# A four-layer graph network on one core: the source stage's three engine orders rewritten, its attribute scans parted, and the attributes' mean moved to the destination stage

## The chip, the core and the metric

The kernel runs on one core of a Trainium2 chip. The core has five instruction streams: TensorE (PE; its weight loads are listed apart as PEld), VectorE (DVE), ScalarE (ACT), GpSimd (POOL) and SyncE (SP, which here only issues DMA transfers). Each stream runs in its own order and waits for the others through semaphores. The metric is the device time of one execution in microseconds (us), lower is better.

## The reference, cut to what matters

There are 100,000 nodes with 128 features, and 50,000 edges sorted by destination. Four layers follow each other; after each of them `x = layernorm(x + layer(x))`.

```python
# layer 1: three hops over the edges, then one matrix
Z1 = spmm(x); Z2 = spmm(Z1); Z3 = spmm(Z2)      # segment_sum(w[:, None] * Z[src], dst)
x  = layernorm(x + concat(x, Z1, Z2, Z3) @ W0 + b0)
# layer 2: an MLP fed with each node's edge attributes (48 columns)
out1 = segment_sum(attr, dst)
out2 = where(has, segment_max(attr, dst), 0)
out3 = out1 / maximum(cnt, 1)                   # the mean
h    = relu(concat(x, out1, out2, out3, u) @ W1 + b1)
x    = layernorm(x + (h @ W2 + b2 + x))
# layer 3: attention over the edges with a skip matrix; layer 4: one weighted hop
```

A node with no incoming edge has zeros in Z1 to Z3 and in out1 to out3; only nodes that are some edge's destination need the attribute terms.

## The kernel before, in words

All work goes in groups of 512 rows (T = 4 tiles of 128). The 50,000 edges make EG = 98 groups; SL = 4 buffer slots `s` are used in turn, and one loop iteration covers four groups, so the edge loops have EI = 25 iterations. The helper `steps(eng, n, (stage, lag), ...)` writes one engine's program: in every step, for group g, it issues each stage in the order listed, for group g minus that stage's lag. So the lists given to `steps` are the hand-written order of each engine, and one "step" is one group.

The program runs through these stages, one after another: an index preparation; the node stage, in which all 100,000 nodes go through the layers as if they had no edges, while the first two hops run beside it; the **source stage** (98 groups), where the third hop is made and nodes that have edges get layers 1 to 3 in their role as sources, and the attribute sums and maxima are made by running scans; the **destination stage** (98 groups, in reverse order), where layer 2 is made again with the attributes for destination nodes; the attention; and the last hop with the output.

In the source stage, for group g:

- POOL (line 803) gathers 4 x 128 rows of the second hop into `gat` (`z_gather(2)`) and 4 x 128 rows of the input into `xg` (`x_gather`). The buffers have four slots; a gather waits for PE to have turned the tile of four groups before. After the last gather POOL issues 44 scatters of a code table (`codes`, line 804), and then, after waits for the X1 stores, starts the gathers of the destination stage (`dst_gather`).
- DVE (lines 2032 to 2034) weighs the gathered rows (L1924), scans them (`z_scan`, L1945, in from PSUM), sums squares for three layer norms (`power`, L1897), applies them (`norm`, L1909 and L1912), makes the second residual (`layer2`, L1979), and treats the attributes: the running sum (L2020), the running maximum (L2022), both in `attr_scan`, and the mean (`attr_mean`, L2029).
- PE (lines 1148 and 1149) turns tiles (L970) and multiplies: `chain_b1` and `chain_d1` turn the first and second normed tile, `z_turn` and `x_turn` the gathered ones, `chain_a` is the four-part product of layer 1 (L1020, L1025), `chain_b2` and `chain_c` the MLP (L1065, L1080), `chain_d2` the skip product (L1123).
- ACT (lines 1369 to 1371) makes squares (L1265), square roots (L1279), relu (L1336), copies out of PSUM (L1255) and PSUM seeds (L1244).
- SP loads the two earlier hops, row masks and attributes (`attr_load` has four transfers, one of them the row `inv` of reciprocal counts), and stores the three normed tiles, ATT (sums and maxima) and MNT (means).

In the destination stage PE multiplies the turned rows, ATT and MNT by three parts of W1 in one accumulation (`chain_b2("d")`, L1065, L1067, L1068). DVE's list there is line 2057, SP's loads are `att_load`.

The two DVE lines of the attribute scans, which depend on the group before through the last column:

```python
dve.tensor_tensor_scan(att_e[s][0:AF, :], f2B[s][0:AF, :], atr_e[s][0:AF, :],
                       att_e[s - 1][0:AF, G - 1:G], ALU.mult, ALU.add)
dve.tensor_tensor_scan(att_e[s][AM:AK, :], fmB[s][AM:AK, :], atr_e[s][AM:AK, :],
                       att_e[s - 1][AM:AK, G - 1:G], ALU.min, ALU.max)
```

## Time and profile before

| what | value |
|---|---|
| time, median of 3 runs | 6279.33 us (6278.2 to 6283.3) |
| the profiled execution's own time | 6277.28 us |
| its span, first to last instruction | 6275.5 us |
| mean granted TensorE clock | 0.875 of full speed |
| busy: PE, DVE, ACT, POOL | 4503.8, 4371.1, 3114.7, 4344.4 us |
| source stage: first gather to last gather on POOL | 1993.6 to 3066 us |
| destination stage: first gather on POOL | 3127.0 us |

The profile tells for each engine which instructions ran when, and, for idle time just before an instruction, which event ended it ("<-releaser"; "issue" means that it waited for nothing that the profile shows). A group's "mean ns" is the mean duration of one instruction. DVE instructions overlap a little at their ends, so what one costs on DVE is read from start to start.

### The profile page before, as it was taken

The page shows a single profiled execution, that of the slowest core. Times are in us where ns is not written, and L with a number is a line of the kernel's source. Part 1 is how long each engine was busy: PE and PEld are TensorE (multiplying, and loading weights), DVE is VectorE, ACT ScalarE, POOL GpSimd, SP SyncE. Part 2 cuts the span into 40 slices and gives each one's busy share as a digit, 9 for nine tenths or more (in the row PEclk, how much of TensorE's full clock was granted, in tenths as well). Part 3 has the DMA queues.
Part 4 walks back from the last instruction along what each step waited for, and adds up shares of the span by engine and source line. Part 5 has one row for each costly group of instructions (what it writes and reads, how often), then busy time and mean ns, then how long its engine had stood idle before and what let it go on. Part 6 is the DMA issues. An engine that isn't in the chain of part 4 may idle for free. (4 is left out here: it accounts for less than half of the span.)

```text
span 6275.5 us, 102230 instructions
## 1 busy us (share of the span) xinstructions
PE 4503.8 (72%) x25328; PEld 3191.3 (51%) x25328; DVE 4371.1 (70%) x8168; ACT 3114.7 (50%) x6471; POOL 4344.4 (69%) x4339
## 2 busy tenths in 40 slices
PE   1079899997886999999889999978887884432200
PEld 0057688886665777777744444444444442211100
DVE  8966799987886888888733334369999995753300
ACT  0057688885664555555533333348888883110000
POOL 0056677777777777777766666657777776777777
PEclk9999999999999999999999999988888885555555
DMA  1033588887897999999755555534444446953311
GB/s 30 7 87 109 169 250 248 252 239 226 283 287 218 257 262 263 263 262 263 212 163 164 167 165 163 164 113 115 113 115 115 115 116 204 328 171 96 96 42 40
DMA packets 896637, 1090.56 MB, mean 174 GB/s; under 512 B 137109, under 2 KB 543521, under 8 KB 895492
## 3 DMA queue, kind: packets, MB, share of 16 engines
q1 hardware_dynamic: 757158, 816.08, 43.4%
q0 software_dynamic: 137984, 221.55, 13.8%
q10 hardware_dynamic: 1344, 51.38, 2.1%
q14 instruction: 113, 0.93, 0.0%
q8 instruction: 38, 0.62, 0.0%
HBM read 652.84 MB, written 497.99 MB: 183 GB/s over the span
## 5 line engine op out<-in xcount | busy, mean ns | idle before, releaser
L970 PE MATMUL bank<-ident,gat 128*128 128x128 f32 x2352 | 430.5, 312 | 627.7 <-DVE zT L1945 551.5
L1080 PE MATMUL bank<-W2s,hT 128*128 128x128 f32 x6272 | 777.1, 277 | 77.6 <-ACT hT L1336 77.6
L1065 PE MATMUL bank<-x1T,W1x 128*128 128x512 f32 x1568 | 773.1, 605 | 30.5 <-ACT x1T L1255 26.9
L1080 PEld LDWEIGHTS bank<-W2s,hT 128*128 128x128 f32 x6272 | 733.9, 192 | 103.6 <-ACT hT L1336 102.2
L970 PEld LDWEIGHTS bank<-ident,gat 128*128 128x128 f32 x2352 | 298.3, 161 | 776.2 <-issue 582.5
L1265 ACT ACTIVATE mbuf<-t 128x512 f32<-128x512 f32 x490 | 310.1, 633 | 711.2 <-DVE t L1979 440.8
L1336 ACT ACTIVATE hT<-bank,b1u 128x512 f32<-128x512 f32 x784 | 491.4, 677 | 245.2 <-PE bank L1068 236.3
L1924 DVE TENSOR_TENSOR gat<-gat,pays 128x512 f32<-128x512 f32 x392 | 270.6, 690 | 425.5 <-DMA gat<-X,pays 366.5
L970 PE MATMUL bank<-ident,x 128*128 128x128 f32 x3136 | 487.1, 278 | 107.6 <-DVE x L1912 84.9
L722 POOL DMA_INDIRECT gat<-X,d_x x392 | 392.8, 1002 | 222.2 <-issue 222.2
L735 POOL DMA_INDIRECT Y<-x,d_out x392 | 405.0, 1033 | 176.4 <-issue 116.4
L970 PEld LDWEIGHTS bank<-ident,x 128*128 128x128 f32 x3136 | 366.4, 142 | 313.3 <-DVE x L1912 169.6
L722 POOL DMA_INDIRECT gat<-X,s_src x392 | 402.5, 1027 | 161.9 <-issue 161.6
L722 POOL DMA_INDIRECT gat<-Z2E,pays x392 | 416.2, 1062 | 121.0 <-issue 120.7
L1945 DVE TENSOR_TENSOR_SCAN zT<-fB,zT,bank 128x512 f32<-128x512 f32 x392 | 498.2, 1271 | 2.2 <-PE bank L970 2.2
L722 POOL DMA_INDIRECT x<-in_x_rows,s_src x392 | 415.9, 1061 | 119.5 <-issue 119.5
L722 POOL DMA_INDIRECT gat<-in_x_rows,pays x392 | 378.2, 965 | 148.5 <-issue 117.5
L756 POOL DMA_INDIRECT VQ<-s_v,s_q x392 | 396.4, 1011 | 119.4 <-issue 119.4
L722 POOL DMA_INDIRECT gat<-X,pays x392 | 385.2, 983 | 129.3 <-issue 118.6
L749 POOL DMA_INDIRECT pays<-PAY,s_q x392 | 373.1, 952 | 146.3 <-issue 109.3
L722 POOL DMA_INDIRECT gat<-Z1E,pays x392 | 377.8, 964 | 119.6 <-issue 100.3
L2046 DVE TENSOR_TENSOR zT<-bank,ffB 128x512 f32<-128x512 f32 x98 | 67.8, 692 | 540.8 <-PE bank L970 540.8
(366 smaller groups left out, 11529.4 us busy)
## 6 DMA issues: line engine op xcount, KB each, us to landing
X<-x SPq DMA_DIRECT2D x588, 256.0 KB, 3.0
fB<-row_s_same SPq DMA_DIRECT2D x392, 256.0 KB
Y<-x SPq DMA_DIRECT2D x294, 256.0 KB, 3.8
xT<-in_x_fm SPq DMA_DIRECT2D x196, 256.0 KB
ffB<-rows_last_notlast SPq DMA_DIRECT2D x98, 512.0 KB
out_rows<-Y ACTq DMA_DIRECT2D x28, 1792.0 KB, 10.4
Z1T<-zT SPq DMA_DIRECT2D x98, 256.0 KB
Z1E<-zE SPq DMA_DIRECT2D x98, 256.0 KB
```

What stands on the lines that cost most here:

```text
L722: pool.indirect_dma_start(out=tile[:, t, 0:width], out_offset=None, in_=table, in_offset=bass.IndirectOffsetOnAxis(ap=index[t], axis=0)).t ...
L735: pool.indirect_dma_start(out=table, out_offset=bass.IndirectOffsetOnAxis(ap=index[t], axis=0), in_=rows[t], in_offset=None, bounds_check= ...
L749: pool.indirect_dma_start(out=pays[:, c, :], out_offset=None, in_=PAY, in_offset=bass.IndirectOffsetOnAxis(ap=s_q[:, c:c + 1], axis=0)).th ...
L756: pool.indirect_dma_start(out=VQ, out_offset=bass.IndirectOffsetOnAxis(ap=s_q[:, c:c + 1], axis=0), in_=s_v[:, c:c + 1], in_offset=None, b ...
L970: mm = pe.transpose(dst[:, t, :], tiles[t], ident[:, :])
L1065: mm = pe.matmul(bH[h][:, :, :], W1x[:, cols], x1T[s][:, :], start=True, stop=kind != "d")
L1080: mm = pe.matmul(bMLP[:, t, :], hT[h][s][:, t * P:(t + 1) * P], W2s[:, h, :], start=False, stop=h == HC - 1, skip_group_check=True)
L1265: act.activation(sq[k % 3][s % 2], [bT1, t2[s], bSK, t2[s]][k][:, :, :], ACT.Square).then_inc(S(f"squared{k}", s), 1)
L1336: a = act.activation(hT[h][s][:, :], flat(bH[h]), ACT.Relu, bias=b1u[:, h:h + 1])
L1924: dve.tensor_tensor(gat[s][:, :, 0:P], gat[s][:, :, 0:P], pays[:, bass.ds(g, T), 1].bitcast(F32).rearrange("p (t a) -> p t a", a=1).to_bro ...
L1945: dve.tensor_tensor_scan(zT[s][:, :], fB[s][:, :], flat(bIN), zT[s - 1][:, G - 1:G], ALU.mult, ALU.add).then_inc(S("scanned", s), 1)
L2046: dve.tensor_tensor(zT[s][:, :], flat(bTR), f2B[s][:, :], ALU.mult).then_inc(S("x2sel", s), 1)
```

## The change

The source stage is given new orders on PE, ACT and DVE; the two scans of `attr_scan` become two stages (`attr_scan` for the sum, `attr_max` for the maximum) with `layer2` between them; `norm2` moves from the start of the next step (lag 4) to the end of its step (lag 3), ahead of the third norm. The mean is no longer made, stored (MNT) or fed (`inv`) in the source stage: the destination stage loads the row `inv` in place of MNT, into the buffers of `x1`, and makes the mean there (`att_mean`). SP waits for all X1 stores before the destination loads. The list of the whole change, lines that only renumber a semaphore's base included:

```diff
@@ -83,10 +83,10 @@
 
         AFTER = {
             "ld_z": ("ld_x", NI * 16), "ld_x2d": ("ld_z", EI * 32),
-            "ld_last": ("ld_attr", EI * 64), "ld_own": ("ld_x2d", EI * 32),
+            "ld_last": ("ld_attr", EI * 48), "ld_own": ("ld_x2d", EI * 32),
             "st_x2d": ("st_zT", EI * 32), "st_att": ("st_z2", 2 * EI * 16),
             "decayed": ("x2d", EI), "centred": ("attr_sums", EI),
-            "delta": ("attr_mean", EI), "t3": ("x2sel", EI), "fin_sum": ("agg", EI),
+            "delta": ("att_mean", EI), "t3": ("x2sel", EI), "fin_sum": ("agg", EI),
             "q_mm": ("skip", NI + EI), "k_mm": ("x2_turned", NI + 2 * EI), "v_mm": ("hidden", NI + 2 * EI),
             "alpha": ("mlp", NI + 2 * EI), "skip_e": ("x1_turned", NI + 2 * EI), "agg_turned": ("mm1", NI + EI),
             "q_out": ("x1T", NI + 2 * EI), "decay": ("relu", NI + 2 * EI), "weight": ("x2T", NI + EI),
@@ -123,7 +123,6 @@
         Y = dram("Y", [N_X + E_PAD, P])
         ZT = [dram(f"Z{k}T", [P, E_PAD]) for k in (1, 2)]
         ATT = dram("ATT", [AK, E_PAD])
-        MNT = dram("MNT", [AF, E_PAD])
         X2DT = dram("X2DT", [P, E_PAD])
 
         PAIRS = {p: dram("rows_" + "_".join(p), [2, E_PAD]) for p in (
@@ -267,6 +266,7 @@
 
         att, mnt, atr = ([flat(a) for a in z] for z in zin)
         x2d = fB
+        inv_d = [flat(x) for x in x1s]
         xg, atr_e, att_e = x4, atr, [flat(z) for z in zE]
         xs, qT, prod, dlt, dec, elt = x1T, hT[0], hT[1], att, mnt, atr
         aw, av, den, agg, aggn, own = [flat(t) for t in xT], f2B, zT, [flat(t) for t in zE], x2T, xT
@@ -582,22 +582,20 @@
 
 
             def attr_load(i, s):
-                if void(sp, i, s, ("ld_attr", i, 64)):
+                if void(sp, i, s, ("ld_attr", i, 48)):
                     return
                 g = i * SL + s
-                reuse(sp, "st_att", s, i, 32)
+                reuse(sp, "attr_sums", s, i)
                 sp.dma_start(atr_e[s][0:AK, :], attr_fm[:, epos(g)]).then_inc(S("ld_attr", s), 16)
                 row_load(f2B[s], ROWS["same"], g, S("ld_attr", s), 0, AF)
                 row_load(fmB[s], ROWS["samem"], g, S("ld_attr", s), AM, AF)
-                row_load(fmB[s], ROWS["inv"], g, S("ld_attr", s), 0, AF)
 
             def attr_store(i, s):
-                if void(sp, i, s, ("st_att", i, 32)):
+                if void(sp, i, s, ("st_att", i, 16)):
                     return
                 g = i * SL + s
-                ready(sp, "attr_mean", s, i)
+                ready(sp, "attr_sums", s, i)
                 sp.dma_start(ATT[:, epos(g)], att_e[s][0:AK, :]).then_inc(S("st_att", s), 16)
-                sp.dma_start(MNT[:, epos(g)], atr_e[s][0:AF, :]).then_inc(S("st_att", s), 16)
 
             all_slots(sp, "st_zT", 2 * EI * 16)
             all_slots(sp, "st_z2", 2 * EI * 16)
@@ -625,7 +623,9 @@
 
 
             all_slots(sp, "mm1", NI + EI)
-            all_slots(sp, "st_att", EI * 32)
+            all_slots(sp, "st_att", EI * 16)
+
+            all_slots(sp, "st_x1_", (NI + EI) * 16)
 
             def att_load(i, s):
                 if void(sp, i, s, ("ld_att", i, 32), ("ld_last", i, 16)):
@@ -633,7 +633,7 @@
                 g = edge_group(i, s, True)
                 reuse(sp, "hidden", s, ci("d", i))
                 sp.dma_start(att[s][0:AK, :], ATT[:, epos(g)]).then_inc(S("ld_att", s), 16)
-                sp.dma_start(mnt[s][0:AF, :], MNT[:, epos(g)]).then_inc(S("ld_att", s), 16)
+                row_load(inv_d[s], ROWS["inv"], g, S("ld_att", s), 0, AF)
                 reuse(sp, "x2d", s, i)
                 pair_load(ffB[s], ("last", "notlast"), g, S("ld_last", s))
 
@@ -1060,6 +1060,7 @@
                 prior(pe, "relu", s, c)
                 if kind == "d":
                     ready(pe, "ld_att", s, i, 32)
+                    ready(pe, "att_mean", s, i)
                 for h in range(HC):
                     cols = slice(h * P, (h + 1) * P)
                     mm = pe.matmul(bH[h][:, :, :], W1x[:, cols], x1T[s][:, :], start=True, stop=kind != "d")
@@ -1145,8 +1146,8 @@
             all_slots(pe, "z_rows", 2 * EI)
             all_slots(pe, "x2T", NI)
 
-            steps(pe, EI, (of("s", chain_b1), 2), (of("s", chain_a), 1), (of("s", chain_b2), 2),
-                  (of("s", chain_d1), 4), (z_turn(2), 0), (x_turn, 0), (of("s", chain_c), 3), (of("s", chain_d2), 4), peeled=1)
+            steps(pe, EI, (of("s", chain_b1), 2), (of("s", chain_a), 1), (of("s", chain_b2), 2), (z_turn(2), 0),
+                  (x_turn, 0), (of("s", chain_d1), 4), (of("s", chain_c), 3), (of("s", chain_d2), 4), peeled=1)
             all_slots(pe, "x2T", NI + EI)
             all_slots(pe, "x_src", EI)
             all_slots(pe, "scanned", 3 * EI)
@@ -1366,9 +1367,9 @@
                 reuse(act, "mm1", s, ci("s", i))
                 evac(xT[s][:, :, :], bBK[:, :, :], S("x_src", s))
 
-            steps(act, EI, (square("s", 0), 1), (std("s", 0), 1), (relu("s"), 2), (seed_mm1("s"), 0), (x2_out("s"), 4),
-                  (x_src, 0), (square("s", 1), 3), (seed_mlp("s"), 2), (std("s", 1), 3), (x1_out("s"), 1), (square("s", 2), 4),
-                  (std("s", 2), 4), peeled=1)
+            steps(act, EI, (square("s", 0), 1), (std("s", 0), 1), (relu("s"), 2), (x2_out("s"), 4), (x_src, 0),
+                  (seed_mm1("s"), 0), (square("s", 1), 3), (square("s", 2), 4), (std("s", 1), 3), (std("s", 2), 4),
+                  (x1_out("s"), 1), (seed_mlp("s"), 2), peeled=1)
 
             steps(act, EI, (x1_out("d"), 0), (square("d", 1), 2), (seed_mlp("d"), 1), (std("d", 1), 2), (relu("d"), 1),
                   peeled=1)
@@ -2012,30 +2013,38 @@
 
             def attr_scan(i, s):
 
-                if void(dve, i, s, ("attr_sums", i, 1)):
-                    return
-                ready(dve, "ld_attr", s, i, 64)
-                reuse(dve, "st_att", s, i, 32)
+                if void(dve, i, s):
+                    return
+                ready(dve, "ld_attr", s, i, 48)
+                reuse(dve, "st_att", s, i, 16)
                 prior(dve, "attr_sums", s, i)
                 dve.tensor_tensor_scan(att_e[s][0:AF, :], f2B[s][0:AF, :], atr_e[s][0:AF, :],
                                        att_e[s - 1][0:AF, G - 1:G], ALU.mult, ALU.add)
+
+            def attr_max(i, s):
+
+                if void(dve, i, s, ("attr_sums", i, 1)):
+                    return
+                prior(dve, "attr_sums", s, i)
                 dve.tensor_tensor_scan(att_e[s][AM:AK, :], fmB[s][AM:AK, :], atr_e[s][AM:AK, :],
                                        att_e[s - 1][AM:AK, G - 1:G], ALU.min, ALU.max).then_inc(S("attr_sums", s), 1)
 
-            def attr_mean(i, s):
-                if void(dve, i, s, ("attr_mean", i, 1)):
-                    return
-                ready(dve, "attr_sums", s, i)
-                dve.tensor_tensor(atr_e[s][0:AF, :], att_e[s][0:AF, :], fmB[s][0:AF, :], ALU.mult
-                                  ).then_inc(S("attr_mean", s), 1)
-
-            steps(dve, EI, (norm2("s"), 4), (z_weigh(2), 0), (power("s", 0), 1), (norm1("s"), 1), (z_scan(2), 0),
-                  (layer2("s"), 3), (power("s", 1), 3), (attr_scan, 0), (power("s", 2), 4), (attr_mean, 0),
+            steps(dve, EI, (z_weigh(2), 0), (power("s", 0), 1), (norm1("s"), 1), (z_scan(2), 0), (attr_scan, 0),
+                  (layer2("s"), 3), (attr_max, 0), (power("s", 1), 3), (power("s", 2), 4), (norm2("s"), 3),
                   (norm("s", 2, lambda s: bSK, x3, "ln3_out", x3_free), 4), peeled=1)
             all_slots(dve, "mm1", NI + EI)
-            all_slots(dve, "st_att", EI * 32)
+            all_slots(dve, "st_att", EI * 16)
             dve.memset(x2d[SL - 1][:, :], 0.0).then_inc(S("carry0"), 1)
             dve.wait_ge(S("carry0"), 2)
+
+            def att_mean(i, s):
+
+                if void(dve, i, s, ("att_mean", i, 1)):
+                    return
+                ready(dve, "ld_att", s, i, 32)
+                reuse(dve, "hidden", s, ci("d", i))
+                dve.tensor_tensor(mnt[s][0:AF, :], att[s][0:AF, :], inv_d[s][0:AF, :], ALU.mult
+                                  ).then_inc(S("att_mean", s), 1)
 
             def x2_select(i, s):
 
@@ -2054,7 +2063,8 @@
                 dve.tensor_tensor_scan(x2d[s][:, ::-1], fmB[s][:, ::-1], zT[s][:, ::-1], x2d[s - 1][:, 0:1],
                                        ALU.mult, ALU.add).then_inc(S("x2d", s), 1)
 
-            steps(dve, EI, (x2_select, 3), (layer2("d"), 2), (x2_carry, 3), (power("d", 1), 2), (norm2("d"), 2), peeled=1)
+            steps(dve, EI, (x2_select, 3), (layer2("d"), 2), (x2_carry, 3), (power("d", 1), 2), (att_mean, 0), (norm2("d"), 2),
+                  peeled=1)
 
 
             def att_scores(i, s):
```

## Rows read from the trace of the kernel before

**Rows 1.** The page: busy time of each engine over the span.

```profile
PE 4503.8 (72%) x25328; PEld 3191.3 (51%) x25328; DVE 4371.1 (70%) x8168; ACT 3114.7 (50%) x6471; POOL 4344.4 (69%) x4339
```

**Rows 2.** Busy time by stretch, steady source stage: PE, PEld, DVE, ACT, POOL.

```profile
core 0: us, PE busy (x) PEld busy (x) DVE busy (x) ACT busy (x) POOL busy (x), PEclk, DMA share, GB/s
2100.00:3050.00 950.00, 871.50 (x6393) 730.63 (x6392) 827.07 (x1262) 520.98 (x1092) 737.24 (x694) 1.00 0.96 263
```

**Rows 3.** Waits, 2300 to 2900 us (source stage): total us, times, longest.

```profile
PE bank L970 <- DVE x L1912: 25.1, 53, 0.6
PE bank L1123 <- ACT x2T L1255: 24.4, 54, 0.5
...
DVE ln2vr L1897 <- ACT mbuf L1265: 37.6, 54, 0.7
```

**Rows 4.** Groups of POOL instructions, 1990 to 3066 us: busy, mean ns, idle before.

```profile
L722 POOL DMA_INDIRECT gat<-Z2E,pays x392 | 416.2, 1062 | 121.0 <-issue 120.7 <-PE bank L970 0.3
L722 POOL DMA_INDIRECT x<-in_x_rows,s_src x392 | 415.9, 1061 | 119.5 <-issue 119.5
```

**Rows 5.** Timeline of POOL in one source step: start, duration, instruction, idle before.

```profile
2302.18 1.54 POOL L722 DMA_INDIRECT x<-in_x_rows,s_src  x1 [0.30 <-issue]
2304.02 0.99 POOL L722 DMA_INDIRECT x<-in_x_rows,s_src  x1 [0.30 <-issue]
2305.32 1.07 POOL L722 DMA_INDIRECT x<-in_x_rows,s_src  x1 [0.30 <-issue]
2306.70 1.39 POOL L722 DMA_INDIRECT x<-in_x_rows,s_src  x1 [0.30 <-issue]
2308.39 0.94 POOL L722 DMA_INDIRECT gat<-Z2E,pays  x1 [0.30 <-issue]
...
2310.89 0.94 POOL L722 DMA_INDIRECT gat<-Z2E,pays  x1 [0.30 <-issue]
2312.13 0.94 POOL L722 DMA_INDIRECT gat<-Z2E,pays  x1 [0.30 <-issue]
2313.38 1.55 POOL L722 DMA_INDIRECT x<-in_x_rows,s_src  x1 [0.30 <-issue]
```

**Rows 6.** Timeline of DVE in the same step.

```profile
2301.70 1.27 DVE L2020 TENSOR_TENSOR_SCAN zE<-ffB,zE,zin 48x512 f32<-48x512 f32 x1
2302.98 1.28 DVE L2022 TENSOR_TENSOR_SCAN zE<-ffB,zE,zin 48x512 f32<-48x512 f32 x1
...
2304.89 0.67 DVE L2029 TENSOR_TENSOR zin<-zE,ffB 48x512 f32<-48x512 f32 x1
2305.49 0.16 DVE L1909 RECIPROCAL ln3rs<-ln3sd 128x4 f32<-128x4 f32 x1
...
2306.58 0.69 DVE L1912 TENSOR_TENSOR x<-t,ln2rs 128x512 f32<-128x512 f32 x1
...
2309.76 1.27 DVE L1945 TENSOR_TENSOR_SCAN zT<-fB,zT,bank 128x512 f32<-128x512 f32 x1
2310.95 0.67 DVE L1979 SCALAR_TENSOR_TENSOR t<-x,bank 128x512 f32<-128x512 f32 x1
```

**Rows 7.** Timeline of POOL at the start of the destination stage.

```profile
3127.02 0.99 POOL L722 DMA_INDIRECT gat<-X,d_x  x1 [0.31 <-issue]
...
3147.61 0.94 POOL L722 DMA_INDIRECT gat<-X,d_x  x1 [0.30 <-issue]
```

**Rows 8.** Timeline of PE there: the turn of the third destination group.

```profile
3156.65 0.66 PE L970 MATMUL bank<-ident,gat 128*128 128x128 f32 x4 [0.69 <-DMA gat<-X,d_x]
```

**Rows 9.** Waits, 3200 to 4000 us (destination stage).

```profile
DVE zT L2046 <- PE bank L970: 444.5, 80, 5.8
...
POOL gat L722 <- issue: 187.1, 322, 2.5
```

**Rows 10.** DMA issues, 2300 to 2900 us: transfers, KB each.

```profile
ffB<-row_inv SPq DMA_DIRECT2D x54, 96.0 KB
MNT<-zin SPq DMA_DIRECT2D x53, 96.0 KB
```

## The prediction

> **What bounds the kernel now.** The page first: PE, DVE and POOL are all busy 69 to 72% of the span [rows 1], so no engine is the bound everywhere and the stage has to be read by itself. In the steady source stage [rows 2] PE is busy 92% and DVE 87% of the time, the clock is at its higher level, 2.4 GHz (1.00), and the 16 DMA engines are busy 96% at 263 GB/s. The waits come next [rows 3]: 53 steps in 600 us, so one group takes 11.32 us. PE waits twice in a step, 25.1/53 = 0.47 us for DVE's second norm and 24.4/54 = 0.45 us for ACT's copy; DVE waits 37.6/54 = 0.70 us for ACT's square ahead of its second sum. DVE is full but for ACT's round trips: it sets the step, and PE waits for it.
>
> That is what the change goes at. But who sets when the destination stage can begin is another question, and for that POOL's rows are read. Its 784 gathers took 416.2 + 121.0 + 415.9 + 119.5 = 1072.6 us, and all idle time but 0.3 us is issue time [rows 4]: POOL waited for nobody. That is 10.94 us a group, only 0.38 under PE's and DVE's step. After them come the code scatters, and the first destination gather at 3127.02 follows with 0.31 us of issue time alone [rows 7], so POOL comes to it late, not PE. The third destination tile is turned at 3156.65 after PE waited 0.69 us for its gather [rows 8]. So POOL is the longest queue through this stage; DVE and PE are hardly behind it.
>
> What is POOL's time made of? Undisturbed, gathers start (2312.13 - 2308.39)/3 = 1.247 us apart [rows 5], which for eight is 9.97 us. The other 0.97 us of each group is gathers that take longer, and timeline against timeline shows which. The gather at 2302.18 starts inside the running sum (2301.70 to 2302.97 [rows 6]) and ends at 3.72, 0.75 us after the sum's end; that at 2313.38 does the same a step later. The one at 2306.70 starts inside the second norm (to 2307.27) and ends 0.82 after it; the one at 2305.32 is held a little by the reciprocal at 2305.49. The one at 2310.89 starts inside the third-hop scan, which reads PSUM, and takes its 0.94 us. So **a gather that starts during a DVE instruction whose operands are all in SBUF is caught until that instruction ends**, and needs some 0.75 us more; one that started before it goes through. The gather after a caught one starts 0.30 us later, 1.05 us after the catching instruction's end.
>
> A rule speaks against such catches: the Trainium skill's page "SBUF — State Buffer", section "Who interferes with whom", says that an instruction with two SBUF inputs contends with GpSimd instructions that read SBUF, and infers that `tensor_tensor` does not hold up descriptor generation. By its inference the 0.97 us would not come from DVE and POOL would run at 9.97 us a group; rows 5 and 6 disagree with the inference and fit the same section's "fully blocks" until the other finishes.
>
> **The change part by part.** *DVE's step* loses the mean, 2305.49 - 2304.89 = 0.60 us from start to start [rows 6], and, with the maximum now between `layer2` and the second sum, the 0.70 us wait (the square is made beside a scan of 1.28 us): 11.32 - 1.30 = 10.02 us. The wait for the first square root stays. *PE's step* loses up to both its waits, since `chain_d1` comes after two more turns and its input is made a norm earlier, and ACT copies its output before seeding: 11.32 - 0.47 - 0.45 = 10.40 us. *ACT*, busy 55% [rows 2], has room in any order: nothing. *SP and DMA*: two transfers of 96 KB go from each group [rows 10]. At 263 GB/s a step moves 2.98 MB in 0.96 x 11.32 = 10.87 us of DMA time; without 0.197 MB of them 10.15 us. SP issues ten transfers a step in place of twelve; the new waits on the scans instead of on the mean or a store come earlier in the step: nothing lost. So PE, DVE and DMA could all step at about 10.4 us, a gain of 0.9 us a group. None of it counts unless POOL's 10.94 us shrinks as well, as POOL issues the same 784 gathers.
>
> *POOL under the new order.* Before, the two attribute scans stood back to back. A gather caught by the sum let the next one start 1.05 us into the maximum's 1.28, with 0.24 us left, so the second delay was 0.05 us (2304.02 took 0.99). Now `layer2` lies between; its input is PSUM, so it catches nothing, but it moves the maximum to 0.60 us (the mean's start-to-start time, for an instruction as long) after the sum's end, so it runs from 0.60 to 1.88 after that end. The next gather starts at 1.05, is caught, and ends at 1.88 + 0.75 = 2.63 in place of 1.05 + 0.94 = 1.99: 0.64 us late. The first catch itself costs 0 to 1.06 us by where the gather starts; 0.60 us was paid in rows 5, and since with starts 1.247 us apart some sums would catch none, I take 0.50. The second norm and the weighing, some 0.69 us each and now with the third norm (PSUM, catches nothing) between them, can catch one each for up to 0.5; before it was 0.45 for the pair [rows 5]. Both stand a gather or more behind the maximum, and I take 0.10, as most gathers start clear of two short instructions. The mean's own small catch goes. Sum: 0.50 + 0.64 + 0.10 = 1.24 us, against 0.97. Bounds: 0.54 (the sum's catch alone, 0.04 beside it) and 1.70 (1.06 + 0.64).
>
> POOL's group: 9.97 + 1.24 = 11.21 us, and 98 of them 1098.6 us, 26.0 more than now. That is above 10.40, so PE and DVE, made faster, wait for gathers.
>
> *The start of the destination stage.* A part of a late POOL is taken back: the third gather ended at 3148.55 [rows 7] and PE turned it 8.1 us later [rows 8], with the first ATT and MNT loads of that stage in flight; in the new kernel those are done before POOL comes. Between 0 and 8.1 us; I take half, -4.
>
> *The destination stage itself.* The mean costs DVE about 0.6 us a group, but DVE waits 444.5/80 = 5.6 us a group there for PE [rows 9]: nothing. Uncovered it would cost 98 x 0.6 = 59 us. Queued behind its wait for the loads are the second norm and what follows; PE's `chain_b2` waits for it, one step later. SP loads `inv` in place of MNT, 96 KB each: nothing. The mean can catch POOL for up to 0.5 us, but POOL has (187.1 - 322 x 0.30)/80 = 1.1 us idle a group there [rows 9]: nothing. The wait for the X1 stores is behind stores that SP issued before the last Y stores: nothing.
>
> **Sum.** 26.0 - 4 = +22 us. The profiled execution took 6277.28 us (span 6275.5), so 6299.3; the median shown is 2.05 us above it, so 6301.
>
> **The rivals.**
>
> *One catch only (faster).* `layer2` waits for `chain_c`, which on PE now comes after `x_turn`, and `x_turn` waits for a gather. If that holds `layer2` back by more than 0.45 us (1.05 - 0.60), the maximum begins after the second gather has started and misses it; much more than 0.9, and it catches the next. For it: POOL-bound, PE stands at `x_turn`. Against: the wait must stay in a window under half a microsecond wide. Then 9.97 + 0.54 = 10.51 us a group, 1030.0 in all, -42.6 - 4: 6233 us.
>
> *PE's step (faster still).* If the long gathers come from the transfers taken away and not from DVE's operands, POOL runs at 9.97 and PE's 10.40 sets the stage: 1019.2 us, -53.4 - 4: 6222 us. For it: DMA at 96%. Against: the ends of the catching instructions in rows 5 and 6 fit to 0.1 us. This is where the skill's inference, above, would lead.
>
> *The same lateness as before (no change).* Catches shift but sum to 0.97 again: -4 us, 6275 us. For it: only 0.7 us of DVE's SBUF work leaves a step that is barely shorter, so gathers meeting it at random would be caught as often.
>
> *Every sum caught early (slower).* 1.70 us, 11.67 a group: +71 - 4, 6346 us.
>
> **How the numbers follow.** A measurement of this kernel can tell 0.2%, some 12.6 us, from no change. Two catches near my terms, 0.51; the same lateness, 0.22; one catch, 0.17; PE's step, 0.10. So slower 0.51, same 0.22, faster 0.27. The range reaches from the one-catch case to the upper bound of the two catches, 6233 to 6346; outside lie PE's step and the edges, under 0.2. The likeliest case alone: 6292 to 6346.
>
> **What would show it.** Right: POOL's 784 source gathers take about 1100 us with issue time alone before them; in each step one gather of about 1.5 us ends 0.75 us after the sum, the next but for nothing between ends 0.75 us after the maximum; DVE's weighing waits for the gathers' DMA, or PE's `x_turn` does; the step is 11.2 us although DVE's own work is 10.0. Wrong: gathers at a mean under 1.0 us, a step at 10.4 to 10.6 us, or the first destination gather before 3110 us. In the destination stage PE's step should stay as it was, with the mean in DVE's idle time.

## The result, and the profile after

The changed kernel takes 6296.87 us (median of 13 runs, 6289.13 to 6303.18) against 6283.15 us (13 runs) for the kernel before: ratio 1.0021, 95% interval 1.0013 to 1.003, slower by 13.7 us. The forecast was 6301. The prediction put at 12.6 us what a measurement can tell from no change, so the direction is clear of that by little. The profiled execution of the changed kernel took 6292.1 us with a span of 6290.3, 14.8 more than before by either.

POOL's gathers of the source stage, the groups that answer to [rows 4] (columns: count, busy us, mean ns, idle before and what ended it):

```profile
L722 POOL DMA_INDIRECT x<-in_x_rows,s_src x392 | 449.4, 1147 | 119.4 <-issue 119.4
L722 POOL DMA_INDIRECT gat<-Z2E,pays x392 | 405.7, 1035 | 119.5 <-issue 119.5
```

Together 1094.0 us, or 11.16 a group, against 1072.6 and 10.94: 21.4 us longer, and still nothing but issue time ahead of any gather. Now one step of the two timelines, POOL's first (answering to [rows 5]):

```profile
2314.49 1.79 POOL L722 DMA_INDIRECT x<-in_x_rows,s_src  x1 [0.30 <-issue]
2316.58 1.59 POOL L722 DMA_INDIRECT gat<-Z2E,pays  x1 [0.31 <-issue]
```

and DVE's (answering to [rows 6]):

```profile
2314.27 1.25 DVE L2021 TENSOR_TENSOR_SCAN zE<-ffB,zE,zin 48x512 f32<-48x512 f32 x1
2315.45 0.65 DVE L1980 SCALAR_TENSOR_TENSOR t<-x,bank 128x512 f32<-128x512 f32 x1
2316.13 1.28 DVE L2029 TENSOR_TENSOR_SCAN zE<-ffB,zE,zin 48x512 f32<-48x512 f32 x1
```

The sum ends at 2315.52 and the gather that started in it at 2316.28, 0.76 us later. The next starts inside the maximum (to 2317.41) and ends at 2318.17, again 0.76 later. Two catches, 0.85 and 0.65 us late, where the same two scans in [rows 5, 6] cost 0.60 and 0.05. When the two timelines are matched over all 98 groups, 83 gathers start in the sum and are late by 0.70 us on average (0.60 a group), 86 in the maximum by 0.59 (0.52 a group), and everything else adds 0.05. Before, the sum gave 0.46 a group, the maximum 0.04, and the second norm, the weighing and the mean 0.43 together.

PE now waits for POOL's gathers, and DVE for PE. The waits from 2300 to 2900 us (total us, times, longest), answering to [rows 3]:

```profile
DVE t L1980 <- PE bank L1081: 47.5, 17, 5.8
...
PE bank L970 <- DMA x<-in_x_rows,s_src: 39.2, 20, 3.6
```

The waits of [rows 3] (for the second norm, ACT's copy, the square) are gone, as the change has it; in their place PE waits for gathered rows in every third step or so, and `layer2` behind it. The steady stretch of [rows 2], again:

```profile
2100.00:3050.00 950.00, 878.86 (x6452) 766.92 (x6451) 785.74 (x1189) 543.14 (x1104) 743.08 (x680) 0.97 0.89 246
```

DVE's busy share fell from 87 to 83% and the DMA share from 96 to 89%, and the time did not fall. The start of the destination stage on POOL, answering to [rows 7],

```profile
3147.22 0.99 POOL L722 DMA_INDIRECT gat<-X,d_x  x1 [0.30 <-issue]
...
3167.73 0.95 POOL L722 DMA_INDIRECT gat<-X,d_x  x1 [0.30 <-issue]
```

and the third turn on PE, answering to [rows 8]:

```profile
3170.17 0.66 PE L970 MATMUL bank<-ident,gat 128*128 128x128 f32 x4 [0.51 <-DMA gat<-X,d_x]
```

The first gather is 20.2 us later than before, the third turn 13.5. The two differ because before the change PE, not POOL, came to the destination stage last. PE's last product of the source stage, its first turn of a destination group and its first layer-2 product there, before:

```profile
3138.10 2.07 PE L1123 MATMUL bank<-WsI,x2T 128*128 128x128 f32 x8 [0.68 <-ACT x2T L1255]
3142.33 1.12 PE L970 MATMUL bank<-ident,gat 128*128 128x128 f32 x4 [2.16 <-ACTq L318]
...
3148.40 2.04 PE L1065 MATMUL bank<-x1T,W1x 128*128 128x512 f32 x2 [3.10 <-DMA zin<-MNT]
```

and the last product and the first turn after:

```profile
3125.36 2.08 PE L1124 MATMUL bank<-WsI,x2T 128*128 128x128 f32 x8 [0.68 <-ACT x2T L1256]
3154.83 1.09 PE L970 MATMUL bank<-ident,gat 128*128 128x128 f32 x4 [27.39 <-DMA gat<-X,d_x]
```

Before, POOL had issued the first group's four gathers by 3131.8, PE was in the source stage until 3140.2, and by its row the first turn waited for no gather. Now PE is through 12.7 us earlier, at 3127.4, and waits 27.39 us for the gathers.

### The profile page after: what moved, and what is told of

It reads as the page before. It is cut to its first block and busy times, and to the rows that moved or that the text cites. A ratio compares the mean times of both kernels' runs of the same rounds, so it can differ in the third digit from the quotient of the medians.

```text
span 6290.3 us, 102075 instructions
## 1 busy us (share of the span) xinstructions
PE 4504.0 (72%) x25328; PEld 3221.9 (51%) x25328; DVE 4361.1 (69%) x8168; ACT 3134.6 (50%) x6471; POOL 4368.4 (69%) x4339
## 3 DMA queue, kind: packets, MB, share of 16 engines
q0 software_dynamic: 137984, 221.55, 13.6%
## 5 line engine op out<-in xcount | busy, mean ns | idle before, releaser
L1081 PE MATMUL bank<-W2s,hT 128*128 128x128 f32 x6272 | 797.1, 282 | 76.3 <-ACT hT L1337 76.3
L1081 PEld LDWEIGHTS bank<-W2s,hT 128*128 128x128 f32 x6272 | 754.4, 197 | 101.9 <-ACT hT L1337 100.4
L722 POOL DMA_INDIRECT x<-in_x_rows,s_src x392 | 449.4, 1147 | 119.4 <-issue 119.4
L722 POOL DMA_INDIRECT gat<-Z2E,pays x392 | 405.7, 1035 | 119.5 <-issue 119.5
L756 POOL DMA_INDIRECT VQ<-s_v,s_q x392 | 400.6, 1022 | 119.5 <-issue 119.5
L722 POOL DMA_INDIRECT gat<-Z1E,pays x392 | 378.8, 966 | 119.5 <-issue 100.6
## 6 DMA issues: line engine op xcount, KB each, us to landing
out_rows<-Y ACTq DMA_DIRECT2D x28, 1792.0 KB, 10.2
```

The source lines that it names most:

```text
L722: pool.indirect_dma_start(out=tile[:, t, 0:width], out_offset=None, in_=table, in_offset=bass.IndirectOffsetOnAxis(ap=index[t], axis=0)).t ...
L756: pool.indirect_dma_start(out=VQ, out_offset=bass.IndirectOffsetOnAxis(ap=s_q[:, c:c + 1], axis=0), in_=s_v[:, c:c + 1], in_offset=None, b ...
L1081: mm = pe.matmul(bMLP[:, t, :], hT[h][s][:, t * P:(t + 1) * P], W2s[:, h, :], start=False, stop=h == HC - 1, skip_group_check=True)
```

## The experiments

Ratios are to the kernel before, beside which each ran; a difference of two ratios times 6285 us gives the us between two kernels. "POOL" is the two groups of its 784 source gathers, busy and idle, over 98; "first" is the start of the first destination gather.

| kernel | median us | ratio | interval | POOL, us a group | first, us |
|---|---|---|---|---|---|
| before | 6283.15 | 1 | | 10.94 | 3127.0 |
| the change | 6296.87 | 1.0021 | 1.0013 to 1.003 | 11.16 | 3147.2 |
| scans side by side | 6227.99 | 0.9912 | 0.9896 to 0.9929 | 10.52 | 3083.1 |
| before, scans parted | 6327.84 | 1.0073 | 1.0056 to 1.009 | 11.49 | 3179.0 |
| codes later | 6271.28 | 0.9983 | 0.9973 to 0.9992 | 11.15 | 3118.1 |
| no maximum | 6196.77 | 0.9862 | 0.9846 to 0.9878 | 10.17 | 3052.9 |
| maximum as reductions | 6266.65 | 0.9968 | 0.9956 to 0.9981 | 10.84 | 3113.3 |
| both scans as reductions | 6193.46 | 0.985 | 0.9833 to 0.9866 | 10.11 | 3042.6 |
| the mean's move alone | 6280.20 | 0.9983 | 0.9973 to 0.9992 | 10.86 | 3116.4 |
| side by side, old PE and ACT orders | 6293.34 | 1.0008 | 0.9998 to 1.0017 | 11.05 | 3137.3 |
| side by side, all codes later | 6218.81 | 0.989 | 0.9873 to 0.9906 | 10.52 | 3056.4 |
| side by side, half the codes later | 6209.48 | 0.9878 | 0.9861 to 0.9894 | 10.52 | 3058.6 |
| weighing early | 6271.23 | 0.9978 | 0.9968 to 0.9987 | 10.88 | 3122.5 |
| no mean | 6298.69 | 1.0022 | 1.0012 to 1.0032 | 11.24 | 3152.4 |

**Scans side by side.** The changed kernel with one move in DVE's order:

```diff
-  (z_scan(2), 0), (attr_scan, 0), (layer2("s"), 3), (attr_max, 0), (power("s", 1), 3),
+  (z_scan(2), 0), (layer2("s"), 3), (attr_scan, 0), (attr_max, 0), (power("s", 1), 3),
```

> The changed kernel with its two attribute scans side by side again (layer2 ahead of both), all else as changed. Theory (each scan with all operands in SBUF catches a gather that starts inside it, and the split lets the maximum catch one more): the second catch shrinks to about 0.05 us, POOL goes from 11.16 us a group to about 10.6, its 784 gathers from 1094 to about 1040 us, and the time falls by about 50 us, to near 6245 us, which is 35 us under the kernel before. Rival A (the long gathers do not hang on where the maximum stands): POOL stays within 0.1 us of 11.16 a group, the time within 10 us of the changed kernel. Rival B (the lateness per group is a constant of DVE's total work in SBUF): 10.94 to 11.16 a group, time between that of the two kernels, 6275 to 6297 us.

Two gathers of a step on POOL, then the two scans on DVE:

```profile
2311.67 1.52 POOL L722 DMA_INDIRECT gat<-Z2E,pays  x1 [0.30 <-issue]
2313.50 1.00 POOL L722 DMA_INDIRECT gat<-Z2E,pays  x1 [0.30 <-issue]
```

```profile
2311.17 1.27 DVE L2021 TENSOR_TENSOR_SCAN zE<-ffB,zE,zin 48x512 f32<-48x512 f32 x1
2312.46 1.28 DVE L2029 TENSOR_TENSOR_SCAN zE<-ffB,zE,zin 48x512 f32<-48x512 f32 x1
```

The second gather starts 0.24 us before the maximum's end and costs 0.06, as the theory has it. POOL takes 419.6 + 119.4 + 372.2 + 119.5 = 1030.7 us, and the time falls by 0.0109 x 6285 = 69 us against the changed kernel, some 20 more than expected. In the stretch from 2100 to 3000 us

```profile
2100.00:3000.00 900.00, 876.17 (x6505) 758.47 (x6506) 792.28 (x1199) 523.55 (x1111) 691.55 (x685) 1.00 0.94 262
```

PE is busy 97%, and the kernel beats both. Rivals A and B fall.

**Before, scans parted.** Nothing of the change but the split, for which the maximum becomes a stage of its own:

```diff
-  (power("s", 1), 3), (attr_scan, 0), (power("s", 2), 4), (attr_mean, 0),
+  (power("s", 1), 3), (attr_scan, 0), (power("s", 2), 4), (attr_max, 0), (attr_mean, 0),
```

> The kernel before with only the split: the maximum is a stage of its own and the second sum of squares (a reduction, under which no gather was seen to be caught) stands between sum and maximum. Theory: a second catch of 0.4 to 0.65 us a group appears, POOL goes from 10.94 to 11.35 to 11.6 us a group, and the time grows by 30 to 60 us, to 6315 to 6345 us. Rival (the position of the scans does not matter, the changed kernel is slower for another part of the change): POOL stays at 10.9 to 11.0, the time within 10 us of the kernel before.

POOL and DVE in one step:

```profile
2309.62 1.54 POOL L722 DMA_INDIRECT gat<-Z2E,pays  x1 [0.30 <-issue]
2311.46 1.85 POOL L722 DMA_INDIRECT gat<-Z2E,pays  x1 [0.30 <-issue]
```

```profile
2309.14 1.27 DVE L2020 TENSOR_TENSOR_SCAN zE<-ffB,zE,zin 48x512 f32<-48x512 f32 x1
2310.56 0.69 DVE L1897 TENSOR_REDUCE ln3vr<-sq 128x4 f32<-128x512 f32 x1 [0.15 <-ACT sq L1265]
2311.27 1.28 DVE L2027 TENSOR_TENSOR_SCAN zE<-ffB,zE,zin 48x512 f32<-48x512 f32 x1
```

Each gather ends 0.75 or 0.76 us after its scan; the sum costs 0.61 us a group and the maximum 0.87. POOL goes to 11.49 us a group and the kernel is slower by 0.73%, both as expected, but the second catch is larger than the 0.4 to 0.65 expected; the total fits because the second norm's catch fell from 0.32 to 0.02 us a group. Parting the scans is enough to make the old kernel slower; the rival falls. PE now waits 22.03 us for the first destination gathers, so POOL has become the later one in this kernel too.

**Codes later.** The changed kernel with the 44 code scatters (line 804) moved on:

```diff
-        VG1, VG2, VG3 = 40, 36, 44
+        VG1, VG2, VG3 = 40, 36, 0
```

> The changed kernel with the 44 scatters of the code table that POOL issues between its last source gather and its first destination gather moved into the destination stage; their issue takes about 58 us with what lies between. Theory (POOL's queue alone sets the start of the destination stage): the first destination gather comes 15 to 45 us earlier (held then by the X1 stores and the tail of the source stage, which ends near 3115 us), and the time falls by 15 to 30 us, as the scatters find room in POOL's idle time of the destination stage (about 0.9 us a group). Rival (the tail of PE, DVE or the stores sets the start): the first gather is issued after those all the same, and the time changes by less than 5 us or grows, since the scatters collide with destination gathers.

POOL's first destination gather:

```profile
3118.06 0.94 POOL L722 DMA_INDIRECT gat<-X,d_x  x1 [29.03 <-SPq L318]
```

It starts 29.2 us earlier, and the time falls by 0.0038 x 6285 = 24 us. So POOL's queue does set the start of the destination stage in the changed kernel. Without the scatters the wait for the X1 stores, through SP, takes its place.

**No maximum; the maximum, then both scans, as reductions.** Three kernels on the same place of the changed one (what the instructions signal to other engines is left out here): the maximum's scan gives way to

```diff
-  dve.tensor_tensor_scan(att_e[s][AM:AK, :], fmB[s][AM:AK, :], atr_e[s][AM:AK, :], ...)
+  dve.tensor_copy(att_e[s][AM:AK, 0:1], atr_e[s][AM:AK, 0:1])
```

in the first and to

```diff
+  dve.tensor_reduce(att_e[s][AM:AK, 0:4], atr_e[s][AM:AK, :].rearrange("p (t a) -> p t a", a=P), AX.X, ALU.add)
+  dve.tensor_reduce(att_e[s][AM:AK, 4:8], atr_e[s][AM:AK, :].rearrange("p (t a) -> p t a", a=P), AX.X, ALU.add)
```

in the second; in the third the sum's scan gives way to two such reductions as well.

> The changed kernel with the running maximum left out (a copy of one column stands in its place, so the maxima of the attributes are not computed). It takes about 1.2 us of work off DVE and one catching instruction out of POOL's way. Theory: POOL goes from 11.16 to about 10.5 us a group, its 784 gathers from 1094 to about 1030 us, the time falls by 55 to 65 us to near 6235 us. Rival (the long gathers come from the transfers, or DVE's and PE's orders set the step): POOL stays at 11.0 to 11.2 a group and the time changes by less than 10 us, since neither transfers nor orders are changed.

> The changed kernel with the running maximum's scan replaced by two reductions of the same 48 x 512 rows (the maxima of the attributes are not computed). DVE is busy as long as before, about 1.2 us from start to start, and in the same place, but with an operation under which no gather was seen to be caught. Theory (the kind of instruction catches, not DVE's time or the order): POOL's gathers run as without the maximum, 10.1 to 10.5 us a group in place of 11.16, and the time falls by 60 to 100 us against the changed kernel, to 6197 to 6235 us. Rival (the gain without the maximum was DVE's 1.28 us taken off the step): POOL stays at 11.0 to 11.2 us a group, the time within 15 us of the changed kernel.

> Both scans of the attributes replaced by two reductions each over the same rows (neither sums nor maxima of the attributes are computed); the order is that of the changed kernel and DVE is busy nearly as long. It is to settle why reductions in place of the maximum alone left 10.84 us a group, of which 0.46 was still caught by the sum and 0.39 by the second norm, the weighing and what follows it. Theory (the scans catch; the short instructions catch only gathers that a longer lateness has moved onto them): with both gone POOL goes to 9.97 to 10.4 us a group or fills its four slots and waits for PE, its gathers take 980 to 1020 us, and the time is 6185 to 6230 us. Rival (catches trade places: what the scans leave, the second norm and the weighing take): 10.6 to 10.9 us a group, 6245 to 6275 us.

Without the maximum the time fell by 100 us, more than the theory's 55 to 65, and POOL even waited 17.1 us in all for PE. With two reductions in its place it fell by 33 us only: between theory and rival, so neither size was right. POOL's groups in that kernel:

```profile
L722 POOL DMA_INDIRECT gat<-Z2E,pays x392 | 415.1, 1059 | 119.5 <-issue 119.5
L722 POOL DMA_INDIRECT x<-in_x_rows,s_src x392 | 408.0, 1041 | 119.5 <-issue 119.5
```

There some 100 gathers started in the two reductions and none took over 0.95 us, but the sum still cost 0.46 us a group, and the second norm and the weighing, which cost some 0.05 together in the changed kernel, now cost 0.40. Two accounts were left: that catches trade places for good, or that the remaining scan moves gathers onto the short instructions. The third kernel told them apart:

```profile
L722 POOL DMA_INDIRECT gat<-Z2E,pays x392 | 380.6, 971 | 119.5 <-issue 119.5
L722 POOL DMA_INDIRECT x<-in_x_rows,s_src x392 | 371.0, 946 | 119.5 <-issue 119.5
```

10.11 us a group, in all and in the steady part, with some 0.12 a group of lateness left under the weighing and the second norm: the scans are the cause. And its stretch from 2100 to 2950 us

```profile
2100.00:2950.00 850.00, 838.01 (x6384) 737.97 (x6383) 772.78 (x1344) 537.33 (x1091) 645.00 (x673) 1.00 0.97 272
```

shows DVE busy 91%, more than the 83% of the changed kernel, in a stage 9% shorter. DVE's time was not what the stage waited for. PE is busy 99% there, so it is likely the next bound.

**The mean's move alone.** The changed kernel with all three orders of the kernel before and the scans side by side.

> Only the mean's move to the destination stage, with its loads and stores; PE's, ACT's and DVE's orders of the source stage and the two scans side by side are those of the kernel before. DVE loses 0.60 us a step, DMA 0.2 MB. Theory (POOL's gathers set the stage): POOL goes from 10.94 us a group to 10.7 to 10.9, as only the mean's own small catch goes, and the time falls by 5 to 25 us against the kernel before, to 6258 to 6278 us. Rival (DVE's step or DMA sets the stage): 0.60 us x 98 = 59 us less, 6224 us, or at least 45 less.

POOL 10.86 us a group, the time 0.0017 x 6288 = 11 us less than before: the theory's size, but no test of the theory. From 2100 to 2900 us DVE and PE make a step every 11.19 us, in place of 11.30 before, since part of the mean's 0.60 us came back as a new wait of 0.36 us a step for ACT's square root ahead of the third norm. That wait and PE's first turn of a destination group:

```profile
DVE ln3rs L1910 <- ACT ln3sd L1280: 19.3, 53, 0.4
```

```profile
3131.66 1.12 PE L970 MATMUL bank<-ident,gat 128*128 128x128 f32 x4 [2.16 <-ACTq L318]
```

98 x 0.11 is 11 us as well, PE's source stage ends 10.7 us earlier than before (3129.5), and by its row the turn waited for no gather. So the time followed DVE's and PE's step here, and the rival's 59 us failed only because that step hardly became shorter.

**Side by side, old PE and ACT orders.**

> The kernel with the scans side by side and layer2 ahead of them, but with PE's and ACT's orders of the kernel before. Theory (the stage is set by POOL's catches under DVE's order; the other two orders only have to fit under it): POOL stays at 10.4 to 10.7 us a group, the time within 12 us of 6228 us. Rival (PE's waits for DVE's norm and ACT's copy, 0.47 and 0.45 us a step before, come back and set the step): 10.9 to 11.3 us a group, 6265 to 6300 us.

Its edit: the two `steps` lists of PE and ACT are those of the kernel before. A miss for the theory. From 2300 to 2900 us the waits have

```profile
POOL gat L722 <- issue: 90.4, 211, 1.7
DVE ln3vr L1898 <- ACT sq L1266: 70.6, 52, 1.4
```

DVE waits 70.6/52 = 1.36 us a step for ACT, whose old order makes the third square last, and POOL's issue time holds 1.7 us at its longest in place of 0.3. The catches are few (0.72 us a group in all), yet POOL takes 11.05 us a group. DVE and PE make a step every 11.39 us (2100 to 2900 us); POOL runs at 10.2 until it is some 35 us ahead, with its four slots full, and then keeps their pace. So here the other engines set the step, and the rival's 10.9 to 11.3 holds. Under DVE's new order the new orders of PE and ACT are worth 0.0096 x 6285 = 60 us, but only where POOL's catches leave room for them. Part of that is a mismatch of old and new orders: with all three old (the mean's move alone) the distance to the scans side by side is 0.0071 x 6285 = 45 us.

**Side by side, codes later**, all 44 of them, then 22:

```diff
-        VG1, VG2, VG3 = 40, 36, 44
+        VG1, VG2, VG3 = 40, 36, 0      # then 22
```

> Both repairs together: the scans side by side and the code scatters moved into the destination stage. Theory (the two act on POOL's queue one after the other, so they add): 20 to 26 us less than the kernel with the scans side by side alone, 6202 to 6208 us, 75 to 81 us under the kernel before. Rival (with a faster source stage the tail of PE, DVE and the X1 stores sets the start of the destination stage): less than 12 us gained, 6216 to 6228 us.

> The scans side by side, with 22 of the 44 code scatters moved into the destination stage, not all. With all moved, the first destination gather waited 32.8 us for SP, that is for the X1 stores, so about half of the scatters would have fitted into that wait. Theory (the tail of the source stage, not POOL's queue, sets the start once some 20 scatters are gone): the first destination gather comes within 4 us of that with all moved, 3053 to 3062 us, and the time is the same or up to 8 us less, 6208 to 6222 us, as fewer scatters collide with destination gathers. Rival (POOL's queue still sets the start): half of the gain, 3068 to 3072 us, some 7 us slower than with all moved.

With all of them moved the gain over the scans side by side is 0.0022 x 6285 = 14 us, between theory and rival. POOL's first destination gather:

```profile
3056.43 0.94 POOL L722 DMA_INDIRECT gat<-X,d_x  x1 [32.79 <-SPq L318]
```

It waits 32.8 us for SP, that is for the X1 stores: the tail of the source stage takes over, as the rival says. With 22 moved it starts at 3058.6, 2.2 us later, and the kernel is no slower (0.9878; the intervals of the two overlap): the tail is settled as the bound there. This has the lowest median of the versions that compute everything, 1.2% under the kernel before and 1.4% under the changed one.

**Weighing early.** On the kernel with both repairs:

```diff
-  (z_weigh(2), 0), (power("s", 0), 1), ..., (z_scan(2), 0), (layer2("s"), 3), (attr_scan, 0),
+  (power("s", 0), 2), ..., (z_scan(2), 1), (layer2("s"), 4), (z_weigh(2), 0), (attr_scan, 1),
```

> The kernel with both repairs, and the weighing of the next group's gathered rows moved in DVE's order from the start of the step to between layer2 and the running sum. In the kernel with the scans side by side POOL, by its rows, is no longer the last: in every step DVE's layer2 waits about 0.5 us for PE's chain_c, and PE's turn waits 0.36 us for DVE's weighing, a loop of both engines of 10.4 to 10.5 us. Theory (that loop is the new bound): with the weighing ahead of the scans the loop is some 4 us shorter, the step goes to 10.0 to 10.3 us (DVE's own work, or POOL's 9.97 and a small catch), POOL's 784 gathers to 980 to 1010 us, and the time falls by 15 to 45 us against the kernel with both repairs, to 6170 to 6205 us. Rival A (POOL's catches set 10.42 and the weighing only adds one more SBUF instruction beside the scans): no gain, or 10 to 50 us slower. Rival B (the weighing now waits for its gathers' transfers): DVE waits for the DMA in each step, the time within 10 us.

A miss for the theory: slower by 0.0088 x 6285 = 55 us, in size near rival A's 50 but not by its mechanism, since the catches fell (0.48 us a group). The waits from 2300 to 2900 us:

```profile
DVE t L1980 <- PE bank L1081: 46.6, 54, 1.0
...
PE bank L1066 <- ACT x1T L1256: 40.9, 54, 0.9
...
POOL gat L722 <- PE bank L970: 36.8, 41, 1.0
```

PE waits 40.9/54 = 0.76 us a step for ACT's copy, `layer2` 0.86 us for PE, and POOL for PE's turns: a wait that nobody had named. DVE makes a step every 11.13 us from the start. POOL's pace is 10.4 us a group for the first 28 groups, until it is some 34 us ahead, and 11.1 for the last 56, where it waits for PE's turns to free its slots. So the step of PE and DVE sets this stage, not the catches.

**No mean.** The changed kernel with 4 of the mean's 512 columns:

```diff
-  dve.tensor_tensor(mnt[s][0:AF, :], att[s][0:AF, :], inv_d[s][0:AF, :], ALU.mult)
+  dve.tensor_tensor(mnt[s][0:AF, 0:4], att[s][0:AF, 0:4], inv_d[s][0:AF, 0:4], ALU.mult)
```

> The changed kernel with the attributes' mean in the destination stage cut to 4 of its 512 columns (the mean is left out but for those). Theory (the mean lies in DVE's 5.6 us of waiting for PE there, and costs nothing): the destination stage and the time stay within 8 us of the changed kernel. Rival (the mean, or PE's new wait for it, is on the path): up to 0.6 us x 98 = 59 us less, at least 20 less.

The stretch from 3350 to 4100 us of the changed kernel, then of this one:

```profile
3350.00:4100.00 750.00, 679.78 (x2718) 348.56 (x2719) 332.10 (x525) 236.95 (x451) 511.51 (x511) 1.00 0.53 165
```

```profile
3350.00:4100.00 750.00, 679.88 (x2721) 348.65 (x2721) 299.15 (x525) 236.74 (x451) 511.66 (x510) 1.00 0.53 165
```

DVE is busy 33 us less and nothing else moves; the ratios are 1.0021 and 1.0022. The mean costs nothing there.

## Why the prediction was right, and where its sizes were off

**POOL sets the end of the stage, though no wait names it.** Right for the changed kernel, wrong for the kernel before. In the changed kernel PE stands 27.39 us waiting for POOL's gathers, and scatters taken out of POOL's queue (codes later) brought the next stage forward. In the kernel before, DVE and PE made a step every 11.30 us to POOL's 10.94, as the prediction reads too, and POOL ran ahead: from the end of a group's gathers to its third-hop scan it was 6 us at the eleventh group and 34 at the last. PE came to the destination stage last, 8.4 us after POOL had issued that stage's first gathers. So "POOL comes to it late, not PE" misread [rows 7, 8]: the 8.1 us between the third gather's end and its turn are mostly PE's lateness. The change made PE's end 12.7 us earlier and POOL's queue some 20 later, and what set the end moved from the one to the other. The forecast, which adds all of POOL's delay, came near because the term for the start took some of it back; that the term covers a lead which the prediction denied POOL is luck.

**A gather is caught by a DVE instruction with all operands in SBUF.** The catch is right, and sharper than put: the end of the gather is 0.75 to 0.76 us after a scan's end in every fence above. The class is too wide. Reductions and reciprocals have all operands in SBUF as well, but one input each, and they hold no gather: in the changed kernel 89 gathers started in the third norm's reduction and 69 in a reciprocal, none over 0.96 us, and none over 0.95 started in the reductions put in the maximum's place. Every instruction of the step that caught one has two inputs in SBUF. So the prediction's reading of the gather at 2305.32 is wrong: it started inside the mean (2304.89 to 2305.56 [rows 6]) and ended 0.83 us after it, and the reciprocal held nothing.

In the changed kernel 96 gathers started in the third-hop scan, which is as long but reads PSUM, and none was late. The Trainium skill's page "SBUF — State Buffer", section "Who interferes with whom", has this side of it right: "A DVE instruction with at most one SBUF input, outside the 2-port perf modes, does not contend with GpSimd". Its inference that `tensor_tensor` does not hold up descriptor generation does not carry over to these gathers: in the kernel with reductions in the maximum's place, 75 gathers started in the second norm and 68 of them were late, by 0.35 us on average. These gathers read their indices from SBUF, which the section's rule on two inputs covers; which part of a gather is held no row shows. The words "fully blocks" that the prediction quotes stand there for DVE's 2-port perf mode.

**The terms of POOL's group.** The sum's catch was put at 0.50 and is 0.60; the maximum's 0.64 and is 0.52; the short instructions' 0.10 and is 0.05. The sum, 1.24, is 1.17, closer than its terms because they erred both ways, and the group 11.16 in place of 11.21: +21.4 us for +26.0. The rival of one catch did happen in part: `layer2` waited for `chain_c` in 17 of 54 steps, but 83 and 86 of the 98 scans still caught.

**The start of the destination stage.** This is the mis-sized step: "between 0 and 8.1 us; I take half, -4". POOL's last source gather starts 22.3 us later than before (3087.32 for 3065.02); the way from it to the first destination gather is 2.1 us shorter; and the third turn follows its gather's end by 3170.17 - 3168.68 = 1.5 us in place of 8.1. 22.3 - 2.1 - 6.6 = 13.6, and the turn is 13.5 late. Most of the upper bound was given back, since PE, late by itself before, now waits there for gathers alone. Of the loads that the prediction named, that of MNT did hold PE, for 3.10 us; what else made PE late was its own source stage. The two terms were 4.6 and some 4 us too slow; with both as measured the forecast would have been near 6293, still 4 us from the median, as the end of the kernel came 14.8 us late and not 13.5.

**PE's and DVE's faster steps.** Under POOL's 11.16 the 10.40 and 10.02 us were worth nothing, as predicted. As sums they are only in part borne out. Side by side all engines step at 10.52 us, POOL waiting for nobody and PE busy 97%. Without scans they step at 10.11, with PE busy 99%, so 10.40 was not PE's limit; whether DVE's is 10.02 no run shows. These steps needed the new orders of PE and ACT: with the old ones DVE's and PE's was 11.39.

**The destination stage.** Right: the mean is free, and PE's busy time is 679.8 us in 750, 680.4 before.

**Where reductions taught more than the theory said.** Taking one catch away does not save its average: without the maximum the sum's catch fell from 0.60 to 0.15 us a group, with reductions in its place only to 0.46, while short instructions took 0.40. Where gathers start against DVE's step decides, and that moves with every change of either. The prediction's sum of averages probably came out because its two scans stay at a fixed distance; that was not tried.

## What to carry to other kernels

A queue that never waits can be the next to set the end: compare its pace with its undisturbed pace (here 9.97 us a group) before making any other engine faster. Which of two queues is last is read at the hand-over between stages, from the wait ahead of the first instruction that needs both. Where POOL issues indirect transfers, put DVE's long instructions with two inputs in SBUF side by side, so that one gather pays for two of them, and keep reductions or instructions fed from PSUM elsewhere. After each repair look for the next bound, here PE's step and then the X1 stores.

## What the runs showed of the hardware that was not expected

The granted clock of the source stage fell from 1.00 to a mean of 0.97. Stretches of the changed kernel around one of PE's long waits for gathers (columns as in [rows 2]; the granted clock stands third from the end):

```profile
2292.00:2296.00 4.00, 4.00 (x26) 2.87 (x24) 3.07 (x7) 2.11 (x6) 3.09 (x4) 1.00 0.91 277
2296.00:2299.70 3.70, 0.12 (x2) 0.00 (x0) 3.23 (x4) 1.20 (x3) 2.79 (x4) 0.82 0.91 215
2299.70:2302.00 2.30, 2.25 (x11) 2.25 (x12) 0.00 (x0) 0.24 (x1) 1.69 (x3) 0.50 1.02 283
2302.00:2305.00 3.00, 3.00 (x15) 2.84 (x14) 0.00 (x0) 1.33 (x3) 2.39 (x3) 0.50 0.63 195
2305.00:2308.00 3.00, 2.87 (x25) 2.73 (x25) 2.76 (x4) 1.23 (x3) 2.32 (x3) 0.97 0.17 45
```

PE was busy throughout, then idle 3.6 us, and the next 5.3 us ran at 0.50, that is 1.2 GHz: the eight turns and `chain_c` took

```profile
2299.76 1.97 PE L970 MATMUL bank<-ident,x 128*128 128x128 f32 x8 [3.63 <-DMA x<-in_x_rows,s_src]
2301.52 3.62 PE L1081 MATMUL bank<-W2s,hT 128*128 128x128 f32 x16
```

against 1.04 and 1.95 us with the scans side by side. The many short waits of the kernel before (0.45 us each, [rows 3]) left the clock at 1.00; few long ones did not. This lengthens PE's step just after POOL has made it late; what it adds to the time was not measured by itself.
